# Router logits of the second batch three tiles later, and a new order of the first loads, in a fused attention and mixture-of-experts kernel

## The chip, the cores and the metric

One Trainium2 chip, one of its cores. The number compared is the device time of one execution in microseconds (us). The kernel before took 703.13 us, the median of three runs (702.78 to 705.14). A difference between two versions is read from such runs, and a profile of one execution of each shows where it comes from.

## The reference

Four batches of 512 rows with 512 columns each. First a cross attention whose queries and keys both come from a context `ctx` (so the attention is over context rows) and whose values are the rows of `x` after a layer norm, used along the column axis:

```python
query = einsum('bnc,dc->bnd', ctx, Wq) + bq
key   = einsum('bnc,dc->bnd', ctx, Wk) + bk
attention = softmax(einsum('bnd,bmd->bnm', query, key))
x = x + einsum('bln,bmn->blm', layernorm(x), attention)
h = layernorm(x)
# router: 8 experts, the best 2 of each row, weights renormalised
probs = softmax(h @ gate_w.T);  combine = top2(probs) / sum(top2)
# shared expert of 1408 columns, weighed by its own gate
shared = (silu(h @ sw_gate) * (h @ sw_up)) @ sw_down * sigmoid(h @ shared_gate_w)
# routed experts of 352 columns
moe = sum_e combine[e] * (silu(h @ w_gate[e]) * (h @ w_up[e])) @ w_down[e]
x = x + shared + moe
```

All arrays are float32.

## The kernel before

Every engine has its own instruction stream, written out by hand, and semaphores tie them together; there is no scheduler. An engine works through its stream in order, so a wait holds up all that stands behind it. Large products run as three 16-bit products (`PAIRS`: high by high, high by low, low by high), for which each operand is split into a high half (mostly a copy on ScalarE, ACT) and the remainder (a subtraction on VectorE, DVE).

**The start.** SyncE (SP) issues loads one after the other on its queue: the two projection weights, the rows of batch 0 (`x0_loaded`, 1 MB), the two biases (4 bytes for each of 128 partitions), the router's gate rows (`gw_rows`, 9 rows of 512), the context of batch 1, the rows of batch 1, then the shared expert's weights tile by tile. ACT issues the context of batch 0. TensorE (PE) turns the projection weights and the context (`turn_context`, line 1350), turns the gate rows (line 1472, waits for `gw_loaded`), then projects queries and keys of batch 0 (`project`, line 1357), turns the context of batch 1, and forms the energies (line 1366). DVE meanwhile measures batch 0 (`statistics`, line 900), splits the turned gate rows three ways (lines 1143 to 1152, five small instructions that wait for each other through `gw_step`), normalises batch 0 (line 919, waits for the reciprocal deviation, which GpSimd (POOL) forms at line 591), and then takes the maximum of each energy row (`row_max`, line 930), with which the softmax begins.

**The blocks.** `ffn_block(t)` runs the shared expert on batch t in 11 tiles of 128 columns. On PE each tile j is: the gate product (line 1543, 12 matmuls), the up product (line 1543, 12 matmuls), and the down product of tile j-2 (line 1558, 12 matmuls). ACT forms silu (line 849) and the high half of the hidden tile, DVE the product (line 1271) and the low half. In block 0 ACT and DVE also split the weights of tiles 4 to 10 (lines 826 and 1251), at points listed in `TILES_AT`: tile 8 at (6, "up"), tile 10 at (8, "up"). Tile j's gate product waits for tile j's weights. The staging area holds two tiles, so the load of tile j on SP waits for the split of tile j-2.

**Batch 1 inside block 0.** While block t runs, the attention and routing of batch t+1 are interleaved with it, at points (tile, "gate" | "up" | "down") in tables. For block 0 this is `AT_POINT_FIRST`, which all five engines' streams read; so an entry moves the same stage on PE, ACT and DVE together. At (3, "up") batch 1's normalised rows are split into halves (`halves`). SP then turns the halves by four transposing DMAs into `hT` (`turn_h(1)`, line 506), between the loads of weight tiles 7 and 8. PE's router logits of batch 1 (`router_logits`, line 1420, 32 small matmuls) stand at (5, "up") and wait for all four transposes; nothing before block 1 needs `hT` of batch 1 otherwise. At the same point DVE reads the logits (`read_logits`, lines 993 to 997) and ACT takes the exponential (line 730); at (5, "down") DVE does the routing (`route`, lines 1003 to 1032), whose results are next used in block 1 at (0, "up").

After the four blocks come 39 blocks of routed rows through their experts, which this change does not touch.

Of the kernel before, what the change touches and what calls it, by code (L numbers as in the profile page):

```python
# [13 lines left out]
P = 128  # L14
# [43 lines left out]
    (2, "up"): [("stats2", 0)],  # L58
    (3, "gate"): [("norm2", 0)],
    (3, "up"): [("halves", 0)],  # L60
    (5, "up"): [("logits", 0)],
    (5, "down"): [("route", 0)],
}


# [38 lines left out]
def build_xattn_moe(nc, x, ctx_in, w_q, b_q, w_k, b_k, gate_w, w_gate, w_up, w_down,  # L104
                    sw_gate, sw_up, sw_down, shared_gate_w, out, xs_dram):
    B, S, H = x.shape
    C = ctx_in.shape[2]
    E, _, I = w_gate.shape
    IS = sw_gate.shape[1]
    D = w_q.shape[0]  # L110
    RT = S // P
    KC = H // P
    CC = C // P
    UT = IS // P
    NL = E + 1
# [55 lines left out]
    with ExitStack() as stack:  # L171
        def sb(name, shape, dt):
            return stack.enter_context(nc.sbuf_tensor(name, shape, dt))

        def sem(name):
            return stack.enter_context(nc.semaphore(name))


        bank = [stack.enter_context(nc.psum_tensor(f"bank{i}", [P, 512], F32)) for i in range(8)]
# [7 lines left out]
        def att_bank(b, stage, i):  # L187

            if stage == "h":
                return bank[(2, 0, 1, 3)[i]]  # L190
            if four_banks(b, stage):
                return bank[b * 4 + (2 if stage == "qk" else 0) + i]
            return bank[1] if stage == "assign" else bank[i % 2]
# [62 lines left out]
        def place(b):  # L256
            return borrowed_place if b == 1 else own_place
# [13 lines left out]
        gw_rows = silu_sb[0:NL, :]  # L271
        gw_rest = sb("gw_rest", [P, 2, KC, NL], F32)
        gw3 = sb("gw3", [P, KC, 3, NL], BF16)
        ident = sb("ident", [P, P], F32)
# [10 lines left out]
        logits = sb("logits", [P, RT, NL], F32)  # L285
# [63 lines left out]
        x0_loaded, x1_loaded, x_rest_loaded = sem("x0_loaded"), sem("x1_loaded"), sem("x_rest_loaded")  # L349
        ctx_loaded = sem("ctx_loaded")  # L350
        ctx1_loaded = sem("ctx1_loaded")
        wqk_loaded, bqk_loaded, gw_loaded = sem("wqk_loaded"), sem("bqk_loaded"), sem("gw_loaded")
# [7 lines left out]
        gw_turned, gw_step = sem("gw_turned"), sem("gw_step")  # L360
# [55 lines left out]
        def row_tile(b, i):  # L416
            return rows[b][:, i * H:(i + 1) * H]
# [4 lines left out]
        def _(sp):  # L422
            def load_rows(b, x_sem):
                sp.dma_start(rows[b].rearrange("p (t h) -> p t h", h=H),
                             x[b].rearrange("(t p) h -> p t h", p=P)).then_inc(x_sem, 16)
# [37 lines left out]

            sp.dma_start(wqk[:, 0, :], w_q).then_inc(wqk_loaded, 16)
            sp.dma_start(wqk[:, 1, :], w_k).then_inc(wqk_loaded, 16)
            load_rows(0, x0_loaded)
            sp.dma_start(bqk[:, 0:1], b_q.rearrange("(p a) -> p a", a=1)).then_inc(bqk_loaded, 16)
            sp.dma_start(bqk[:, 1:2], b_k.rearrange("(p a) -> p a", a=1)).then_inc(bqk_loaded, 16)
            sp.dma_start(gw_rows[0:E, :], gate_w).then_inc(gw_loaded, 16)
            sp.dma_start(gw_rows[E:NL, :], shared_gate_w.rearrange("h a -> a h")).then_inc(gw_loaded, 16)  # L470
            sp.dma_start(place(1).ctx_rows, ctx_in[1].rearrange("(t p) c -> p t c", p=P)).then_inc(ctx1_loaded, 16)
            load_rows(1, x1_loaded)

# [419 lines left out]
        def _(dve):  # L893
# [22 lines left out]
            def normalize(which, b):  # L916
                dve.wait_ge(rstd_ready[which], b + 1)
                for i in range(RT):
                    op = nc.vector.tensor_scalar(place(b).normed[:, i, :], row_tile(b, i), mean_var[:, which, i, 0:1],
                                                 rstd[:, which, i:i + 1], ALU.subtract, ALU.mult)  # L920
                    op.then_inc(normed_ready[which], 1)
# [6 lines left out]
            def row_max(b, n):  # L928
                dve.wait_ge(energy_done, RT * b + n + 1)
                nc.vector.tensor_reduce(neg_max[:, n:n + 1], att_bank(b, "energy", n)[:, :], AX.X, ALU.max,  # L930
                                        negate=True).then_inc(max_ready, 1)
# [206 lines left out]
            dve.wait_ge(x0_loaded, 16)  # L1138
            statistics(0, 0)

            gw_ps = bank[5][:, 0:KC * NL].rearrange("p (k e) -> p k e", k=KC)
            dve.wait_ge(gw_turned, 1)
            nc.vector.tensor_copy(gw3[:, :, 0, :], gw_ps).then_inc(gw_step, 1)
            dve.wait_ge(gw_step, 1)
# [5 lines left out]
                                    ALU.subtract).then_inc(gw_step, 1)  # L1150
            dve.wait_ge(gw_step, 4)
            nc.vector.tensor_copy(gw3[:, :, 2, :], gw_rest[:, 1, :, :]).then_inc(gw_step, 1)
            normalize(0, 0)
            row_max(0, 0)
            row_max(0, 1)
            scale_attn(0, 0)
# [183 lines left out]
        def _(pe):  # L1340
            def turn_context(b, c):
                if not first_two(b):
                    if c == 0:
                        pe.wait_ge(ctx_loaded, 16 * b)

                    pe.wait_ge((logits_read, places_read)[c], b)
                elif c == 0:
                    pe.wait_ge((ctx_loaded, ctx1_loaded)[b], 16)
                for i in range(RT):
                    op = nc.tensor.transpose(att_bank(b, "ctx", c)[:, i * P:(i + 1) * P],  # L1350
                                             place(b).ctx_rows[:, i, c * P:(c + 1) * P], ident[:, :])
                op.then_inc(ctx_turned, 1)

            def project(b, i):
                pe.wait_ge(ctxT_ready, CC * b + CC)
                for c in range(CC):
                    op = nc.tensor.matmul(att_bank(b, "qk", i)[:, :], wqkT[:, i, c, :], place(b).ctxT[:, c, :],  # L1357
                                          start=(c == 0), stop=(c == CC - 1))
                op.then_inc(qk_done, 1)
# [9 lines left out]
            def turn_x(b, c):  # L1369
                if c == 0:  # L1370
                    pe.wait_ge(normed_ready[0], RT * b + RT)
                pe.wait_ge(exp_done, RT * b + c + 1)
                for i in range(RT):
                    op = nc.tensor.transpose(att_bank(b, "x", c)[:, i * P:(i + 1) * P],
                                             place(b).normed[:, i, c * P:(c + 1) * P], ident[:, :])
                op.then_inc(x_turned, 1)
# [86 lines left out]
            for i in range(2):  # L1463
                for c in range(CC):
                    op = nc.tensor.transpose(bank[4][:, (i * CC + c) * P:(i * CC + c + 1) * P],
                                             wqk[:, i, c * P:(c + 1) * P], ident[:, :])
            op.then_inc(wqk_turned, 1)
            for c in range(CC):
                turn_context(0, c)
            pe.wait_ge(gw_loaded, 32)  # L1470
            for c in range(KC):
                op = nc.tensor.transpose(bank[5][:, c * NL:(c + 1) * NL], gw_rows[:, c * P:(c + 1) * P],
                                         ident[0:NL, 0:NL])
            op.then_inc(gw_turned, 1)
            pe.wait_ge(wqkT_ready, 1)
            project(0, 0)
            project(0, 1)
            pe.wait_ge(gw_step, 5)
            for c in range(CC):
                turn_context(1, c)  # L1480
            for n in range(RT):
# [3 lines left out]
            project(1, 0)  # L1485
            turn_x(0, 2)
            turn_x(0, 3)
            project(1, 1)
            for c in range(KC):
                turn_attn(0, c)  # L1490
# [182 lines left out]
```

## Time and profile before

| | |
|---|---|
| time, median of three runs | 703.13 us (702.78 to 705.14) |
| the profiled execution's own time | 704.99 us |
| its span, first to last instruction | 703.0 us |
| PE busy | 665.5 us (95%) |
| DVE / ACT / POOL busy | 301.3 / 224.1 / 160.9 us |
| chain that ended last | PE 82%, DVE 7%, DMA 4%, ACT 2% |
| mean granted PE clock | 0.98 of full |

PE is busy nearly throughout, so an interval in which it stands still, or runs at its lower clock, adds to the time unless something else would have held it up anyway. Share of the span says little about single intervals; those are read from the chain of waits and from the timelines of the engines. The stages in us from the span's start: attention of batch 0 to about 48, block 0 to about 160, blocks 1 to 3 to about 458, the experts to the end.

### The profile page before, as it was taken

Reading aid. Unit: us, or ns where it says so; the run is one execution under the profiler, and the core shown is the slowest. Engines: PE = TensorE matmul, PEld = TensorE weight load, DVE = VectorE, ACT = ScalarE, POOL = GpSimd, SP = SyncE. Lnnn points to the kernel's source line nnn. Section 1 sums busy time; section 2 is a strip of 40 time slices with the busy share of each in tenths; the row PEclk is TensorE's granted clock in tenths of the full one; section 3 lists DMA queues with packets and bytes.
Section 4 is the critical chain, followed back from the end, with each engine's and each line's share of the span. In section 5 each row is a group of like instructions: output and inputs, shape, how many; then the busy total and the mean of one; then the engine's idle time right before and its main releaser. Section 6 shows DMA issues by size and latency. Waiting matters only on the chain.

```text
span 703.0 us, 10241 instructions
## 1 busy us (share of the span) xinstructions
PE 665.5 (95%) x3495; PEld 348.4 (50%) x3540; DVE 301.3 (43%) x699; ACT 224.1 (32%) x341; POOL 160.9 (23%) x133
## 2 busy tenths in 40 slices
PE   7989977999999999999999899999999999999991
PEld 5554433444444444444444344456666666666660
DVE  3999544315432536432559763452222222222220
ACT  2545133212630222630445353432222222222220
POOL 2550360003200003200344700012222222222221
PEclk9999997999999999999999999999999999999996
DMA  8530195132530122530167977346566666656632
GB/s 274 187 104 20 49 301 135 50 109 96 147 60 1 28 64 106 137 61 0 36 200 257 310 255 181 94 107 92 92 92 91 92 93 91 93 90 94 90 46 30
DMA packets 116498, 78.29 MB, mean 111 GB/s; under 512 B 79322, under 2 KB 101082, under 8 KB 116451
## 3 DMA queue, kind: packets, MB, share of 16 engines
q1 hardware_dynamic: 104322, 48.77, 28.2%
q0 software_dynamic: 10544, 27.30, 18.1%
q10 hardware_dynamic: 1584, 1.57, 0.7%
q8 instruction: 32, 0.52, 0.3%
q14 instruction: 16, 0.12, 0.1%
HBM read 32.76 MB, written 27.29 MB: 85 GB/s over the span
## 4 chain that ended last, share of the span: by engine, by line
PE 82%; DVE 7%; DMA 4%; ACT 2%; issue 2%; SPq 2%; POOL 1%; ACTq 0%; POOLq 0%
PE bank L1543 26%; PE bank L1591 20%; PE bank L1558 14%; PE bank L1615 10%; PE bank L1400 4%; PE bank L1357 2%; PE bank L1602 2%; PE bank L1366 1%; SPq L506 1%; DMA hT<-L_ffn_w_gate 1%; DVE arena L1245 1%; DMA hT<-hx_odd 1%; DMA silu_sb<-L_ffn_shared_gate_w 1%; DMA out<-staging,token_blk 1%; DVE stats L900 1%
## 5 line engine op out<-in xcount | busy, mean ns | idle before, releaser
L1543 PE MATMUL bank<-hT,arena 128*128 128x512 f16 x1056 | 238.2, 379 | 4.4 <-DVE prod L1271 4.3
L1543 PEld LDWEIGHTS bank<-hT,arena 128*128 128x128 bf16 x1056 | 102.5, 98 | 131.0 <-DVE prod L1271 6.3
L1591 PE MATMUL bank<-arena,hx_odd 128*128 x936 | 152.1, 312 | 0.3 <-issue 0.3
L1558 PE MATMUL bank<-arena,hidden 128*128 128x512 bf16 x503 | 117.8, 384 | 1.4 <-issue 0.2
L1591 PEld LDWEIGHTS bank<-arena,hx_odd 128*128 128x128 f16 x936 | 91.2, 98 | 50.5 <-issue 3.2
L632 POOL DMA_INDIRECT out<-staging,token_blk x39 | 60.6, 1554 | 172.1 <-ACT staging L879 164.0
L1311 DVE TENSOR_TENSOR hidden<-bank,hidden 128x384 bf16<-128x384 f32 x39 | 21.7, 557 | 154.4 <-ACT hidden L871 154.4
L1558 PEld LDWEIGHTS bank<-arena,hidden 128*128 128x128 bf16 x528 | 52.0, 99 | 64.5 <-issue 5.0
L1615 PE MATMUL bank<-arena,hidden 128*128 (+1 forms) x331 | 78.0, 379 | 2.6 <-DVE hidden L1311 1.5
L879 ACT ACTIVATE staging<-bank,w_blk 128x512 f32<-128x512 f32 x39 | 26.8, 687 | 125.6 <-PE bank L1615 125.6
L1271 DVE TENSOR_TENSOR prod<-silu_sb,bank 128x512 f32<-128x512 f32 x44 | 30.1, 684 | 80.4 <-PE bank L1543 74.8
L849 ACT ACTIVATE silu_sb<-bank 128x512 f32<-128x512 f32 x44 | 26.2, 596 | 117.1 <-PE bank L1543 117.0
L843 ACT CAST hidden<-prod 128x512 bf16<-128x512 f32 x44 | 27.0, 618 | 88.2 <-DVE prod L1271 88.2
L1615 PEld LDWEIGHTS bank<-arena,hidden 128*128 128x128 bf16 (+1 forms) x351 | 34.3, 98 | 37.9 <-issue 1.7
L1276 DVE TENSOR_TENSOR hidden<-prod,hidden 128x512 bf16<-128x512 f32 x44 | 35.0, 798 | 28.4 <-ACT hidden L843 28.2
L591 POOL TENSOR_TENSOR rstd<-var_eps,minus_half 128x4 f32<-128x4 f32 x8 | 9.7, 1208 | 155.7 <-DVE var_eps L913 155.5
L1400 PE MATMUL bank<-arena 128*128 128x512 f16 x192 | 43.1, 379 | 0.0
L866 ACT ACTIVATE silu_sb<-bank 128x352 f32<-128x352 f32 x39 | 18.1, 464 | 44.7 <-PE bank L1591 44.7
L1400 PEld LDWEIGHTS bank<-arena 128*128 128x128 f16 x192 | 18.8, 98 | 23.0 <-issue 0.6
L1245 DVE TENSOR_TENSOR arena<-staging,arena 128x1408 bf16<-128x1408 f32 (+1 forms) x14 | 23.5, 1680 | 14.5 <-ACT arena L819 14.2
L819 ACT CAST arena<-staging 128x1408 bf16<-128x1408 f32 (+1 forms) x18 | 25.0, 1395 | 8.8 <-DMA staging<-L_ffn_w_gate 6.5
L1306 DVE TENSOR_TENSOR prod<-silu_sb,bank 128x352 f32<-128x352 f32 x39 | 20.3, 521 | 17.3 <-PE bank L1591 17.3
(183 smaller groups left out, 539.8 us busy)
## 6 DMA issues: line engine op xcount, KB each, us to landing
staging<-L_ffn_w_gate SPq DMA_DIRECT2D x6, 704.0 KB, 4.8
staging<-L_ffn_w_up SPq DMA_DIRECT2D x6, 704.0 KB, 5.7
arena<-x SPq DMA_DIRECT2D x3, 1024.0 KB, 7.9
out<-arena POOLq DMA_DIRECT2D x3, 1024.0 KB, 4.7
staging<-L_ffn_w_down SPq DMA_DIRECT2D x6, 512.0 KB, 4.0
staging<-L_ffn_sw_gate SPq DMA_DIRECT2D x11, 256.0 KB, 3.1
staging<-L_ffn_sw_up SPq DMA_DIRECT2D x11, 256.0 KB, 3.6
staging<-L_ffn_sw_down SPq DMA_DIRECT2D x11, 256.0 KB, 4.5
```

What stands on the lines that cost most here:

```text
L632: nc.gpsimd.indirect_dma_start(out=out[:, :], out_offset=bass.IndirectOffsetOnAxis(ap=token_blk[:, k:k + 1], axis=0), in_=yblk[:, k % 2, : ...
L843: nc.scalar.copy(hidden[:, j % 3, HI, :], prod[:, j % 2, :]).then_inc(hid_hi, 1)
L849: nc.scalar.activation(silu_sb[:, :], gate_ps[:, :], ACT.Silu).then_inc(silu_ready, 1)
L879: nc.scalar.activation(yblk[:, k % 2, :], bank[4 + k % 2][:, :], ACT.Copy, scale=w_blk[:, k:k + 1]).then_inc(y_ready, 1)
L1245: nc.vector.tensor_tensor(arena[:, at + gap:at + gap + n], piece_space[piece_slot(q)][:, 0:n], arena[:, at:at + n], ALU.subtract).then_inc ...
L1271: nc.vector.tensor_tensor(prod[:, j % 2, :], silu_sb[:, :], up_ps[:, :], ALU.mult).then_inc(prod_ready, 1)
L1276: nc.vector.tensor_tensor(hidden[:, j % 3, LO, :], prod[:, j % 2, :], hidden[:, j % 3, HI, :], ALU.subtract).then_inc(hid_lo, 1)
L1400: op = nc.tensor.matmul(att_bank(b, "mix", i)[:, :], place(b).xnT[:, xp, c, i * P:(i + 1) * P], place(b).attnT[:, ap, c, :], start=(c == 0 ...
L1543: op = nc.tensor.matmul(ps[:, :], weights[:, j, wp, kind, c * P:(c + 1) * P], hT[:, t % 2, hp, c, :], start=(c == 0 and s == 0), stop=(c = ...
L1558: op = nc.tensor.matmul(out_ps[i][:, :], hidden[:, j % 3, hp, i * P:(i + 1) * P], weights[:, j, wp, DOWN, :], start=(j == 0 and s == 0), s ...
L1591: op = nc.tensor.matmul(ps[:, 0:I], xT[:, k % X_SLOTS, xp * KC + c, :], arena[:, bass.ds(at + (part_at(0, part) + wp * low_gap(part) + c * ...
L1615: op = nc.tensor.matmul(ps[:, :], hidT[0:n, k % 2, hp, c * P:(c + 1) * P], arena[0:n, bass.ds(at + (DOWN_AT + wp * DN + c * H), H)], start ...
```

## The change

Three edits.

1. In `AT_POINT_FIRST` the entries for batch 1's logits and routing move from tile 5 to tile 8.
2. On PE the first projections (`project(0, 0)`, `project(0, 1)`) stand ahead of the turning of the gate rows, which now go to bank 7 in place of bank 5; the wait for the split gate rows (`gw_step`) moves from ahead of batch 1's context to ahead of `project(1, 1)`, the next user of bank 7. On DVE `normalize(0, 0)` stands ahead of the gate rows' split.
3. On SP the four small loads (two biases, two loads of gate rows) are issued ahead of batch 0's rows.

```diff
-    (5, "up"): [("logits", 0)],
-    (5, "down"): [("route", 0)],
+    (8, "up"): [("logits", 0)],
+    (8, "down"): [("route", 0)],
...
             sp.dma_start(wqk[:, 1, :], w_k).then_inc(wqk_loaded, 16)
-            load_rows(0, x0_loaded)
             sp.dma_start(bqk[:, 0:1], b_q.rearrange("(p a) -> p a", a=1)).then_inc(bqk_loaded, 16)
             sp.dma_start(bqk[:, 1:2], b_k.rearrange("(p a) -> p a", a=1)).then_inc(bqk_loaded, 16)
             sp.dma_start(gw_rows[0:E, :], gate_w).then_inc(gw_loaded, 16)
             sp.dma_start(gw_rows[E:NL, :], shared_gate_w.rearrange("h a -> a h")).then_inc(gw_loaded, 16)
+            load_rows(0, x0_loaded)
...
             statistics(0, 0)
-            gw_ps = bank[5][:, 0:KC * NL].rearrange("p (k e) -> p k e", k=KC)
+            normalize(0, 0)
+            gw_ps = bank[7][:, 0:KC * NL].rearrange("p (k e) -> p k e", k=KC)
             dve.wait_ge(gw_turned, 1)
...
             nc.vector.tensor_copy(gw3[:, :, 2, :], gw_rest[:, 1, :, :]).then_inc(gw_step, 1)
-            normalize(0, 0)
             row_max(0, 0)
...
             for c in range(CC):
                 turn_context(0, c)
-            pe.wait_ge(gw_loaded, 32)
-            for c in range(KC):
-                op = nc.tensor.transpose(bank[5][:, c * NL:(c + 1) * NL], gw_rows[:, c * P:(c + 1) * P],
-                                         ident[0:NL, 0:NL])
-            op.then_inc(gw_turned, 1)
             pe.wait_ge(wqkT_ready, 1)
             project(0, 0)
             project(0, 1)
-            pe.wait_ge(gw_step, 5)
+            pe.wait_ge(gw_loaded, 32)
+            for c in range(KC):
+                op = nc.tensor.transpose(bank[7][:, c * NL:(c + 1) * NL], gw_rows[:, c * P:(c + 1) * P],
+                                         ident[0:NL, 0:NL])
+            op.then_inc(gw_turned, 1)
             for c in range(CC):
                 turn_context(1, c)
...
             turn_x(0, 3)
+            pe.wait_ge(gw_step, 5)
             project(1, 1)
```

The first place is PE in block 0, from batch 1's logits (line 1420) to the end of the block; line 1543 is a tile's gate and up products, line 1558 a down product (x36: the last three). Before:

```order
L1420 MATMUL bank<-gw,hT 128x27 x32
L1558 MATMUL bank<-arena,hidden 128x512 x12
L1543 MATMUL bank<-hT,arena 128x512 x24
L1558 MATMUL bank<-arena,hidden 128x512 x12
L1543 MATMUL bank<-hT,arena 128x512 x24
L1558 MATMUL bank<-arena,hidden 128x512 x12
L1543 MATMUL bank<-hT,arena 128x512 x24
L1558 MATMUL bank<-arena,hidden 128x512 x12
L1543 MATMUL bank<-hT,arena 128x512 x24
L1558 MATMUL bank<-arena,hidden 128x512 x12
L1543 MATMUL bank<-hT,arena 128x512 x24
L1558 MATMUL bank<-arena,hidden 128x512 x36
```

And PE in the same stretch, from the logits to the end of the block, in the changed kernel:

```order
L1420 MATMUL bank<-gw,hT 128x27 x32
L1558 MATMUL bank<-arena,hidden 128x512 x12
L1543 MATMUL bank<-hT,arena 128x512 x24
L1558 MATMUL bank<-arena,hidden 128x512 x12
L1543 MATMUL bank<-hT,arena 128x512 x24
L1558 MATMUL bank<-arena,hidden 128x512 x36
```

Three tiles of products now stand ahead of the logits that stood behind them.

The second place is SP's queue at the start of the program (`arena<-x` is batch 0's rows, then batch 1's; `silu_sb` holds the gate rows, `prod` the context of batch 1):

```order
 L464 DMA arena<-L_xattn_Wq 128x256
 L465 DMA arena<-L_xattn_Wk 128x256
+L466 DMA bqk<-L_xattn_bq 128x1
+L467 DMA bqk<-L_xattn_bk 128x1
+L468 DMA silu_sb<-L_ffn_gate_w 8x512
+L469 DMA silu_sb<-L_ffn_shared_gate_w 1x512
 L424 DMA arena<-x 128x4x512
-L467 DMA bqk<-L_xattn_bq 128x1
-L468 DMA bqk<-L_xattn_bk 128x1
-L469 DMA silu_sb<-L_ffn_gate_w 8x512
-L470 DMA silu_sb<-L_ffn_shared_gate_w 1x512
 L471 DMA prod<-ctx 128x4x256
```

Batch 0's rows are issued four places later.

The third place is DVE at the start, from batch 0's variance to the first row maximum (`gw` and `gw_rest` are the split gate rows, line 919 the normalising):

```order
 L913 TENSOR_SCALAR var_eps<-mean_var 128x4
-L1143 CAST gw<-bank 128x4x9
-L1145 TENSOR_TENSOR gw_rest<-bank,gw 128x36
-L1147 CAST gw<-gw_rest 128x4x9
-L1149 TENSOR_TENSOR gw_rest<-gw_rest,gw 128x36
-L1152 CAST gw<-gw_rest 128x4x9
 L919 TENSOR_SCALAR arena<-arena,mean_var,rstd 128x512 x4
+L1144 CAST gw<-bank 128x4x9
+L1146 TENSOR_TENSOR gw_rest<-bank,gw 128x36
+L1148 CAST gw<-gw_rest 128x4x9
+L1150 TENSOR_TENSOR gw_rest<-gw_rest,gw 128x36
+L1153 CAST gw<-gw_rest 128x4x9
 L930 TENSOR_REDUCE neg_max<-bank 128x1 x2
```

The split of the gate rows moves from between variance and normalising to between normalising and the first row maximum.

## Rows read from the trace of the kernel before

**Rows 1.** Chain of waits, 60 to 165 us: start, us, what.

```profile
104.08 5.76 DMA hT<-hx_odd
...
109.89 1.03 PE bank L1420 x32
110.93 0.22 issue
111.15 4.66 PE bank L1558 x11
...
120.99 2.59 PE bank L1558 x12
```

**Rows 2.** Timeline of PE: start, us, engine, line, what, [idle before <-releaser].

```profile
50.87 0.95 PE L1420 MATMUL bank<-gw,hT 128*128 128x27 bf16 x32
...
109.89 1.03 PE L1420 MATMUL bank<-gw,hT 128*128 128x27 bf16 x32 [8.23 <-DMA hT<-hx_odd]
```

**Rows 3.** Stretches: us, PE busy (x), granted clock, DMA share, GB/s.

```profile
9.40:13.00 3.60, 3.55 (x8) 1.91 (x9) 3.29 (x12) 0.00 (x0) 0.22 (x1) 0.53 1.05 383
111.10:113.00 1.90, 1.85 (x5) 0.75 (x5) 0.58 (x4) 1.21 (x2) 0.00 (x0) 0.50 0.25 86
...
44.50:46.00 1.50, 1.50 (x9) 0.50 1.00 285
```

**Rows 4.** Timeline of SP's queue, 76 to 165 us.

```profile
94.13 12.40 SPq L506 DMA_TRANSPOSE hT<-hx_odd  x4
...
107.75 0.83 SPq L436 DMA_DIRECT2D staging<-L_ffn_sw_down  x1
```

**Rows 5.** DMA issues: KB each, us to landing; from 106.5 to 109, then 4.2 to 5.

```profile
staging<-L_ffn_sw_down SPq DMA_DIRECT2D x1, 256.0 KB, 4.5
...
arena<-x SPq DMA_DIRECT2D x1, 1024.0 KB, 10.1
```

**Rows 6.** Timelines of DVE and ACT, 76 to 165 us.

```profile
113.41 1.76 DVE L1251 TENSOR_TENSOR arena<-staging,arena 128x1536 bf16<-128x1536 f32 x1 [1.66 <-ACT arena L826]
...
119.47 0.18 DVE L1032 TENSOR_TENSOR hx_odd<-chosen,top_inv 128x32 f32<-128x32 f32 x1
121.08 0.69 DVE L1271 TENSOR_TENSOR prod<-silu_sb,bank 128x512 f32<-128x512 f32 x1 [1.43 <-issue]
...
118.93 1.46 ACT L826 CAST arena<-staging 128x1536 bf16<-128x1536 f32 x1
```

**Rows 7.** Timeline of all engines, 0 to 62 us.

```profile
1.72 0.43 SPq L424 DMA_DIRECT2D arena<-x  x1
...
3.69 0.23 SPq L470 DMA_DIRECT2D silu_sb<-L_ffn_shared_gate_w  x1
...
9.45 0.49 PE L1472 MATMUL bank<-ident,silu_sb 9*128 9x9 f32 x4 [2.10 <-DMA silu_sb<-L_ffn_shared_gate_w]
9.60 2.47 DVE L900 BATCH_NORM_STATS2 stats<-arena 128x6 f32<-128x512 f32 x4 [9.60 <-DMA arena<-x]
...
12.60 0.19 DVE L1143 CAST gw<-bank 128x36 bf16<-128x36 f32 x1
12.78 1.05 POOL L591 TENSOR_TENSOR rstd<-var_eps,minus_half 128x4 f32<-128x4 f32 x1 [8.72 <-DVE var_eps L913]
...
13.51 0.18 DVE L1152 CAST gw<-gw_rest 128x36 bf16<-128x36 f32 x1
...
13.86 1.92 DVE L919 TENSOR_SCALAR arena<-arena,mean_var,rstd 128x512 f32<-128x512 f32 x4 [0.17 <-POOL rstd L591]
...
17.06 0.69 DVE L930 TENSOR_REDUCE neg_max<-bank 128x1 f32<-128x512 f32 x1 [1.28 <-PE bank L1366]
...
26.16 2.48 DVE L951 TENSOR_TENSOR arena<-bank,arena 128x512 f16<-128x512 f32 x4 [0.74 <-ACT arena L704]
```

**Rows 8.** DMA queues from 3.5 to 3.9 us: packets, MB, share of 16 engines.

```profile
q10 hardware_dynamic: 149, 0.15, 105.4%
q1 hardware_dynamic: 3, 0.00, 2.2%
```

## The prediction

> **What bounds the kernel now.** I read the page first: PE is busy for 95% of the span and carries 82% of the chain that ended last, so the question is where PE stands still or runs slowly, and whether the edits reach those places. The second view was therefore the chain of waits through block 0. The reader is to see there one transfer, the transposing loads of `hT`, that the chain follows for 5.76 us, then the 32 logits of batch 1, and then a down product of twelve matmuls that takes 4.66 us, where the next one takes 2.59 [rows 1]. The third view, the timeline of PE, gives the stall in full: PE idles 8.23 us ahead of the logits of batch 1, while the logits of batch 0 took 0.95 us and waited for nothing [rows 2]. The fourth, the table of stretches, explains the slow product behind it: the granted clock is 0.50 there, the lower of the two levels, 1.2 GHz, after the idle time [rows 3]. So tile 5 holds one clear loss: a wait, and a cold stretch that the wait leaves behind.
>
> The start is bound otherwise. PE waits 2.10 us for the gate rows [rows 7] and then runs at 0.53 [rows 3]. But by 26.16 us, where DVE takes up the low halves of the attention, the chain has passed to DVE, which is nearly always busy from its first row maximum at 17.06 [rows 7]. What counts at the start is when that first row maximum begins.
>
> **The logits three tiles later.** Before, PE reaches the logits at 109.89 - 8.23 = 101.66 [rows 2], and the down product behind them ends at 111.15 + 4.66 = 115.81 [rows 1]: 14.15 us. Warm and without a wait the two cost 0.95 [rows 2] + 2.59 [rows 1] = 3.54 us. The difference is **10.6 us**: 8.23 of stall, 2.07 of cold down product, 0.3 of cold logits and the gap behind them.
>
> Does the wait come back at the new place? A tile is a gate, an up and a down product, 3 x 2.59 = 7.77 us, so three tiles are 23.3 us and PE arrives at 101.66 + 23.3 = 124.97. Nothing upstream of the transposes moves against the products: but for what the start adds to all of them, SP issues them from 94.13 on as before [rows 4] and they land at 109.85 [rows 1], 15.1 us ahead of PE. The edit gives more delay than the stall needed.
>
> What is late next? Three tiles of products run earlier in time, so their weights must be there. The tightest is tile 8, whose load stands behind the transposes on SP's queue: its last part is issued at 107.75 [rows 4] and lands 4.5 us later [rows 5], at 112.25. ACT's half of the split takes 1.46 us and DVE's 1.76 [rows 6], which makes 115.5. PE reaches the gate product of tile 8 after seven products from 101.66, at 119.8. That leaves 4.3 us. ACT stands at the split for some 5 us with the hidden tile 6 and silu of tile 7 behind it; silu 7 needs a gate product that ends at 114.6, and hidden tile 6 isn't needed before 125.9, so nobody waits for it.
>
> At tile 8 itself the logits end at 124.97 + 0.95 = 125.9. Before, tile 7's split on DVE ended 113.41 + 1.76 - 110.92 = 4.3 us after the logits, and the routing ended at 119.65, 8.7 us after [rows 1, 6]. By the same distances tile 10's weights are ready at 130.2, and PE wants them four products after the logits, at 136.3. The product of tile 9 stands behind the routing on DVE: 134.6 + 0.69 [rows 6] = 135.3, and PE wants it one product later than that, at 138.9. Both fit, with 6.1 and 3.6 us to spare. The routing's results go to block 1, behind two more tiles and the last down products. I cost the moved stage itself at nothing beyond its 0.95 us on PE.
>
> **The start.** The split of the gate rows took 12.60 to 13.69 and lay beside POOL's 1.05 us [rows 7]. Now it stands behind the normalising and lies beside nothing: +1.09 us on DVE. But DVE had 1.28 us of idle time ahead of the first row maximum, waiting for PE [rows 7], and PE loses its 2.10 us wait. With the rows of batch 0 on time, the first row maximum would begin at 13.86 + 1.92 + 1.09 = 16.87, 0.2 us earlier than before.
>
> The rows of batch 0 aren't on time, though. Their issue moves behind four small ones, from an end at 2.15 to one 1.77 us later (3.92 - 2.15) [rows 7]. DVE's whole start hangs on that load, from 9.60 on. From below the delay is 0: between 3.5 and 3.9 SP's queue moved 3 packets while the queue with the context took all the engines [rows 8], so an early issue bought little, and the small loads may use that time. From above it is 1.77. I take 1.0, a bit over the middle, since the rows did begin to move soon after 3.9. The context of batch 1 stands behind the same bytes as before and gets no price.
>
> The Trainium skill speaks against this edit: by its page "DMA: Bandwidth & Descriptors", section "Queues, rings and completion order", the descriptors of one ring are taken in order, so the 256 four-byte pieces of the biases and the gate rows must all be taken up before batch 0's rows. By that rule alone the delay would be the whole 1.77 us or more, and the time about 0.8 us longer than I forecast. The trace agrees as to the order: the gate rows, issued behind batch 0's, came at 9.45, with them. It does not show what the small pieces cost when nothing is ahead of them.
>
> PE now finishes its projections and energies early, and will wait for the first exponentials. Waits of 2.10 and 8.23 us were followed by the lower clock [rows 2, 3, 7]. A cold stretch on the path costs about 2.07 us [rows 1], off the path nothing; PE does little in this stretch that DVE doesn't wait for anyway. I put 0.2 us on it, and keep 0 and 2.07 as its bounds. Sum of the start: -0.2 + 1.0 + 0.2 = **+1.0 us**, between -0.2 and +3.6. DVE and then PE are on the chain without a break from there, so all of it reaches the end.
>
> **The sum.** 10.6 - 1.0 = 9.6 us less. The profiled execution took 704.99 itself (span 703.0 and 2.0 around it), which gives 695.4. It lay 1.86 above the median of the runs, near the slowest of them. One cold stretch more or less is a difference of that size: at 44.5 to 46 the clock was 0.50 as well [rows 3]. From the median the forecast is 703.13 - 9.6 = **693.5 us**.
>
> **The rivals.**
> 1. *The start is dear.* Batch 0's rows come the full 1.77 us late, and PE's idle time ahead of the first exponentials leaves a cold stretch in the projections of batch 1. The start costs 3.6 and the time is 703.13 - 10.6 + 3.6 = 696.1. For it: the 1 MB load is the first thing that DVE waits for. Against it: the projections run beside DVE's work.
> 2. *The stall moves into the weights.* Tile 8's load comes late, and PE waits at its gate product instead. It begins to cost when the load takes over 4.5 + 4.3 = 8.8 us. A load of the start took 10.1 [rows 5], which would cost 1.3 us and, at worst, the same cold stretch: 3.4 of the 10.6, that is 696.9. Against it: 4.5 us was measured while the transposes were still running.
> 3. *Slower than before, by the same place.* ACT takes its work in order. If tile 8's load takes over 8.8 + 9.6 = 18.4 us, PE stands at tile 8 longer than it did at the logits. With a landing after 24 us the wait is 15.2 and the time 703.13 - 9.6 + 15.2 = 708.7. No load in these rows took more than 10.1 us.
> 4. *The edit doesn't remove the wait.* If the transposes came to land when PE asks, not when SP issued them, the stall would go with the logits and only the start would show: 703.13 + 1.0 = 704.1. Against it: PE issues nothing that they wait for after batch 1's halves are ready.
>
> **How the numbers follow.** The forecast has a chance of 0.76, the first rival 0.11, the second 0.07, the third 0.03 and the fourth 0.03. The likeliest case's own range is 692 to 696: the start's bounds, less 0.35 of spread between runs below. The 8-in-10 range is 691.0 to 697.2, which takes in the first two rivals and, below, 1.5 us that a cold stretch fewer (at the start or at 44.5) would give. About what a measurement of this kernel can tell from no change is 0.3%, 2.1 us. Faster by more than that: 0.76 + 0.11 + 0.07 = 0.94. The fourth ends at 704.1, within 0.3%: 0.03 for the same. The third, 708.7, is the 0.03 for slower.
>
> **What would show it.** In the new profile no PE wait of over 1 us between the first down product and block 1, and twelve-matmul down products of 2.59 us throughout; the clock's slice at 105 to 123 us at 9 and not 7. The logits on PE about 3 tiles after the tile-5 products, with no idle time ahead of them. DVE's first statistics at about 10.6 in place of 9.60, the gate rows' split between normalising and the first row maximum, the latter at about 17.9. The forecast is wrong if tile 8's gate product waits for DVE's split, if the logits still wait for `hT`, or if batch 0's rows land after 11.4.

## The result and the profile after

The changed kernel takes 693.99 us (median, 692.27 to 694.44, four runs) against 704.13 for the kernel before (702.78 to 705.23): a ratio of 0.985 with a 95% interval of 0.983 to 0.988. The forecast was 693.5, which is 9.6 us less than the 703.13 that three runs of the kernel before had given; the difference measured is 10.1. The profiled execution took 693.99 itself, its span is 692.1 and was 703.0.

Two lines of the page after, the busy tenths of PE and the granted clock in 40 slices of 17.3 us:

```profile
PE   7989999999999999999998999999999999999991
PEclk9999999999999999999999999999999999999996
```

The slice from 104 to 121 us, in which the kernel before stood still and then ran cold (at the lower of the clock's two levels), is now at 9 on both.

The timeline of PE after, around the logits (start, us, engine, line, what), which answers to [rows 1, 2]:

```profile
118.62 5.34 PE L1543 MATMUL bank<-hT,arena 128*128 128x512 f16 x24
123.80 0.95 PE L1420 MATMUL bank<-gw,hT 128*128 128x27 bf16 x32
124.61 2.75 PE L1558 MATMUL bank<-arena,hidden 128*128 128x512 bf16 x12
127.19 5.34 PE L1543 MATMUL bank<-hT,arena 128*128 128x512 f16 x24
```

No idle time stands ahead of the logits. From one tile's products to the next, with logits and a down product between, it is 127.19 - 118.62 = 8.57 us. The same stretch before, in the timeline of PE:

```profile
96.32 5.34 PE L1543 MATMUL bank<-hT,arena 128*128 128x512 f16 x24
...
115.64 5.34 PE L1543 MATMUL bank<-hT,arena 128*128 128x512 f16 x24
```

That was 19.32 us. The difference, 10.75, is what the moved stage is worth.

What stands on ACT and DVE at the new place, in their timelines after; in brackets the idle time ahead and who ended it:

```profile
112.03 1.47 ACT L826 CAST arena<-staging 128x1536 bf16<-128x1536 f32 x1 [5.56 <-DMA staging<-L_ffn_sw_down]
...
113.53 1.76 DVE L1251 TENSOR_TENSOR arena<-staging,arena 128x1536 bf16<-128x1536 f32 x1 [4.38 <-ACT arena L826]
...
133.30 0.18 DVE L1032 TENSOR_TENSOR hx_odd<-chosen,top_inv 128x32 f32<-128x32 f32 x1
133.52 0.69 DVE L1271 TENSOR_TENSOR prod<-silu_sb,bank 128x512 f32<-128x512 f32 x1
```

ACT does wait for tile 8's load, 5.56 us, and DVE's half of the split ends at 115.29; PE begins that tile's gate product at 118.62, 3.3 us later. The product of tile 9 stands right behind the routing, and nobody waits for it.

The start after, answering to [rows 7], from the timeline of all engines:

```profile
3.35 0.42 SPq L424 DMA_DIRECT2D arena<-x  x1
...
9.75 2.47 DVE L900 BATCH_NORM_STATS2 stats<-arena 128x6 f32<-128x512 f32 x4 [9.75 <-DMA arena<-x]
...
15.85 0.19 DVE L1144 CAST gw<-bank 128x36 bf16<-128x36 f32 x1
...
16.84 1.28 DVE L930 TENSOR_REDUCE neg_max<-bank 128x1 f32<-128x512 f32 x2
...
18.48 1.46 PE L1374 MATMUL bank<-ident,arena 128*128 128x128 f32 x8 [2.12 <-ACT arena L694]
...
19.73 3.39 PE L1357 MATMUL bank<-arena 128*128 128x512 f32 x4
...
26.95 2.48 DVE L951 TENSOR_TENSOR arena<-bank,arena 128x512 f16<-128x512 f32 x4 [1.45 <-ACT arena L704]
```

Batch 0's rows, issued 1.63 us later (3.35 against 1.72), are there at 9.75 instead of 9.60. PE waits 2.12 us for the first exponentials and then runs cold: the granted clock is 0.53 from 19.7 to 23.0, the projection of line 1357 takes 3.39 us, and DVE's low halves begin 0.79 later than before. Yet block 0 starts earlier than before, by 0.9 us. Its first gate product in the timeline of PE, after and before:

```profile
47.38 2.75 PE L1543 MATMUL bank<-hT,arena 128*128 128x512 f16 x12 [0.97 <-DVE hT L963]
```

```profile
48.28 2.75 PE L1543 MATMUL bank<-hT,arena 128*128 128x512 f16 x12
```

Where the 0.79 went, and more, is seen in the timelines of GpSimd (POOL) and DVE, here after:

```profile
29.59 3.10 POOL L586 TENSOR_TENSOR arena<-staging,arena 128x1536 bf16<-128x1536 f32 x1
...
32.27 0.45 DVE L913 TENSOR_SCALAR var_eps<-mean_var 128x4 f32<-128x4 f32 x1
```

and before:

```profile
29.84 3.10 POOL L586 TENSOR_TENSOR arena<-staging,arena 128x1536 bf16<-128x1536 f32 x1
...
31.47 1.49 DVE L913 TENSOR_SCALAR var_eps<-mean_var 128x4 f32<-128x4 f32 x1
```

An instruction of DVE with four elements in each partition, 0.17 us where no split runs beside it, ends when POOL's split of weight tile 1 ends, at 32.7 after and 32.9 before, whenever it began. The start isn't paced by DVE's own work there but by POOL's two splits, which begin with DVE's fourth scaled row (after, that row ends at 23.39 and the first split begins at 23.45; before, 23.63 and 23.70).

### The profile page after: what moved, and what is told of

The parts are those of the page before. It is cut to its first block, busy times and chain, and to the rows that moved or that the text cites. A ratio compares the mean times of both kernels' runs of the same rounds, so it can differ in the third digit from the quotient of the medians.

```text
span 692.1 us, 10286 instructions
## 1 busy us (share of the span) xinstructions
PE 665.4 (96%) x3540; PEld 346.0 (50%) x3540; DVE 300.3 (43%) x699; ACT 224.6 (32%) x341; POOL 160.5 (23%) x133
## 4 chain that ended last, share of the span: by engine, by line
PE 88%; DVE 7%; DMA 2%; issue 1%; ACT 1%; POOL 0%; SPq 0%; POOLq 0%; ACTq 0%
PE bank L1543 30%; PE bank L1591 20%; PE bank L1558 16%; PE bank L1615 11%; PE bank L1400 4%; PE bank L1602 2%; PE bank L1357 2%; PE bank L1366 1%; DMA arena<-x 1%; DVE arena L919 1%; DVE stats L900 1%; DVE arena L1245 1%; DMA out<-staging,token_blk 1%; DVE neg_max L930 0%; DVE stats L1176 0%
## 5 line engine op out<-in xcount | busy, mean ns | idle before, releaser
L1558 PE MATMUL bank<-arena,hidden 128*128 128x512 bf16 x528 | 120.3, 379 | 0.0
L1615 PE MATMUL bank<-arena,hidden 128*128 (+1 forms) x351 | 82.2, 379 | 1.5 <-DVE hidden L1311 1.5
L819 ACT CAST arena<-staging 128x1408 bf16<-128x1408 f32 (+1 forms) x18 | 25.0, 1397 | 10.9 <-DMA staging<-L_ffn_w_gate 7.4
L1306 DVE TENSOR_TENSOR prod<-silu_sb,bank 128x352 f32<-128x352 f32 x39 | 20.3, 521 | 17.3 <-PE bank L1591 17.3
```

The source lines that it names most:

```text
L1558: op = nc.tensor.matmul(out_ps[i][:, :], hidden[:, j % 3, hp, i * P:(i + 1) * P], weights[:, j, wp, DOWN, :], start=(j == 0 and s == 0), s ...
L1615: op = nc.tensor.matmul(ps[:, :], hidT[0:n, k % 2, hp, c * P:(c + 1) * P], arena[0:n, bass.ds(at + (DOWN_AT + wp * DN + c * H), H)], start ...
```

## The experiments

Ratios are to the kernel before, with 95% intervals, from runs on the same chip.

**Only the logits later.** The first edit alone, on the kernel before:

```diff
-    (5, "up"): [("logits", 0)],
-    (5, "down"): [("route", 0)],
+    (8, "up"): [("logits", 0)],
+    (8, "down"): [("route", 0)],
```

> The kernel before with the logits and routing at tile 8, the start as it was. My theory: the whole gain is the wait for the transposes and the cold stretch behind it, so 10.6 to 10.9 us less than before (about 693), no wait on PE ahead of the logits of batch 1, and 2.59 us for the down product behind them. Rival: a good part of the change's gain comes from the start; then this one gains clearly less than the full change, say 8 or under. A cold stretch more or less in either (about 2 us) blurs the difference between single runs.

Measured: 695.3, ratio 0.985 (0.982 to 0.989), that of the full change; no wait ahead of the logits. The rival is out. Its six runs fall into two groups, 693.6 to 693.7 and 696.9 to 697.7. The profile is of the upper one (696.89), and its timeline of the start shows what the old order there can cost:

```profile
10.32 6.63 PE L1357 MATMUL bank<-arena 128*128 128x512 f32 x8
...
18.89 0.69 DVE L930 TENSOR_REDUCE neg_max<-bank 128x1 f32<-128x512 f32 x1 [3.61 <-PE bank L1366]
```

The first projections ran cold throughout (granted clock 0.54 from 10.3 to 16.8) behind a wait of 2.54 us for the gate rows, and the first row maximum waited for PE until 18.89, 1.8 us later than in the profile before.

**Only the start.** The changed kernel with the logits back at tile 5.

> The changed kernel with the logits and routing back at tile 5: only the new order at the start. My theory as predicted: the start costs about 1 us, so 704 to 705; the wait ahead of the logits stays at some 8 us and the down product behind it at 4.66. By the profile of the changed kernel, in which block 0 began 1.0 us earlier than before: 1 us less, about 703. Rival (the start carries the gain): 697 or under.

Measured: 703.93, ratio 0.998 (0.996 to 1.000). The stall is there, in the timeline of PE:

```profile
109.01 1.03 PE L1420 MATMUL bank<-gw,hT 128*128 128x27 bf16 x32 [7.86 <-DMA hT<-hx_odd]
```

The start is worth between nothing and 2.8 us, with no sign of a cost of 1 us. Its down product behind the logits took 3.88, not 4.66: how much of it runs cold differs between these two profiles.

**Tile 6 in place of 8.**

```diff
-    (8, "up"): [("logits", 0)],
-    (8, "down"): [("route", 0)],
+    (6, "up"): [("logits", 0)],
+    (6, "down"): [("route", 0)],
```

> The changed kernel with the logits and routing at tile 6 in place of 8. My theory: the transposes land at a time that doesn't depend on where the logits stand, about 109 us; PE comes to the logits at tile 6 at 100.5 + 7.8 = 108.3, so a wait of 0.5 to 1 us is left, with no fall of the clock, and the time is 0.5 to 1 us above the changed kernel's (694.5 to 695). Rival: the wait moves along with the logits; then 8 us of it and the cold product stay, and the time is 703 or more.

Measured: 694.7, ratio 0.984 (0.981 to 0.987), and no wait at all:

```profile
108.77 0.96 PE L1420 MATMUL bank<-gw,hT 128*128 128x27 bf16 x32
```

The transposes had landed by 108.8 here; my half microsecond was not left, but it was close (with the start alone they landed at 109.01). The landing doesn't move with the logits, and one tile of the three would have done.

**Nothing beside the transposes.** On the kernel before, POOL's stream gets one wait ahead of filling the spare rows and sending batch 0's rows:

```diff
             inverse_deviation(1, 1)
+            pool.wait_ge(hT_in[0], 16 * RT)
             fill_spare()
```

> The kernel before, with GpSimd made to wait for the transposes of batch 1 to have landed before it fills the spare rows and sends batch 0's rows (both of which ran beside the transposes). Theory A: the transposes take 12.4 us to issue because those sends share the DMA engines with them; alone they issue in about 5.4 us, as in block 3, and land at about 103, so that PE waits 1 to 2 us at the logits instead of 8.2 and the time is 6 to 9 us less (694 to 697). Theory B: they are slow by themselves, or by the weight tile ahead of them on the queue; then the wait stays at about 8 and the time at 703 to 705.

Measured: 696.27, ratio 0.987 (0.983 to 0.990). SP's queue and PE, in their timelines (lines after this edit are one higher):

```profile
94.68 7.10 SPq L506 DMA_TRANSPOSE hT<-hx_odd  x4
```

```profile
104.59 0.97 PE L1421 MATMUL bank<-gw,hT 128*128 128x27 bf16 x32 [2.28 <-DMA hT<-hx_odd]
105.41 4.44 PE L1559 MATMUL bank<-arena,hidden 128*128 128x512 bf16 x12
```

Theory A for most of it: the transposes issue in 7.1 us, not in 12.4 [rows 4], and 6 of the 8.2 us of stall go. They were late because POOL's stores ran beside them. The 5.4 us of block 3 didn't come; what holds up the other 1.7 us isn't shown. In this profile, which is of the slowest of the four runs (698.45; the others 695.76 to 696.58), a wait of 2.28 us left most of a cold down product behind it all the same, 4.44 us at a granted clock of 0.59.

**The wait filled.** The changed kernel with 16 transposes of the identity more on PE, between the energies and the first turned rows:

```diff
             for n in range(RT):
                 energy(0, n)
+            for _ in range(16):
+                nc.tensor.transpose(bank[6][:, 0:P], ident[:, :], ident[:, :])
             turn_x(0, 0)
```

> The changed kernel with 16 more transposes of the identity on PE (into a bank that the next projection overwrites) in its wait between the energies and the first turned rows, about 1.7 us of the 2.1. Theory A: the lower clock in the projection of batch 1 (3.4 us where 1.9 is usual) comes from that wait, so the projection is back at 1.9 and the low halves of the attention begin at about 25.7 instead of 26.95; up to 1 us less in time. Theory B: the same as to the clock, but nothing in time (0 plus or minus 0.5), because DVE waits for GpSimd's split of weight tile 1 behind it (its variance of batch 1 ended 32.72, with that split, here and 32.96 before).

Measured: 694.24, ratio 0.985 (0.984 to 0.987). The timeline of PE, then of DVE:

```profile
19.61 1.88 PE L1358 MATMUL bank<-arena 128*128 128x512 f32 x4
```

```profile
25.76 2.48 DVE L952 TENSOR_TENSOR arena<-bank,arena 128x512 f16<-128x512 f32 x4 [0.52 <-ACT arena L705]
...
31.07 1.70 DVE L914 TENSOR_SCALAR var_eps<-mean_var 128x4 f32<-128x4 f32 x1
```

Theory B as to the time. The projection is warm (granted clock 1.00 from 19.6 to 21.4) and DVE comes 1.2 us earlier to its variance, which then takes 1.70 and ends at 32.8, where it ended at 32.7 without the filling. What the warm clock gave, the wait for POOL took. That the filling made the projection warm isn't shown: with the logits at tile 6 the energies ended at the same time as here, PE waited 1.53 us, and the projection took 1.88 without any filling. A second execution of the changed kernel itself says the same of the time. There PE waited 1.23 us and the projection was warm too; DVE's low halves and variance, then PE's first gate product:

```profile
25.70 2.48 DVE L951 TENSOR_TENSOR arena<-bank,arena 128x512 f16<-128x512 f32 x4 [0.52 <-ACT arena L704]
...
31.01 1.70 DVE L913 TENSOR_SCALAR var_eps<-mean_var 128x4 f32<-128x4 f32 x1
```

```profile
47.38 2.75 PE L1543 MATMUL bank<-hT,arena 128*128 128x512 f16 x12 [0.97 <-DVE hT L963]
```

The low halves begin 1.25 us earlier than in the cold profile, and block 0 at the same 47.38.

**Batch 0's rows first again.** The changed kernel without the third edit.

> The changed kernel with the four small loads behind batch 0's rows again (edits 1 and 2 alone). As predicted: batch 0's rows come 1.0 us sooner than with the small loads ahead and the time is about 1 us less. By the profile of the changed kernel, in which batch 0's rows came only 0.15 us later than before: 0.15 less at most, that is no difference. If the gate rows or the biases now come too late for the first projections' outputs (before, the biases landed at 9.0 and 9.9), the energies begin later and nothing is gained.

Measured: 693.74, ratio 0.984 (0.983 to 0.986); the rows came at 9.50. No difference that these runs can tell, as the profile of the changed kernel had it and not as I had predicted.

**The gate rows' split back beside the reciprocal deviation.** The changed kernel with `normalize(0, 0)` behind the split on DVE.

> The changed kernel with the split of the gate rows on DVE back between variance and normalising, beside GpSimd's reciprocal deviation (the turned gate rows are there at 11.9, the variance at 12.9). My theory: the split is hidden again, the first row maximum starts at about 15.8 in place of 16.84, PE's wait ahead of the first turned rows falls from 2.1 to about 1.1 and its clock stays up there. DVE is 1.0 earlier, and the low halves of the attention begin about 1.0 to 2 us earlier than 26.95. Rival: what comes first there doesn't count, because DVE is held up to the end of GpSimd's split of weight tile 1 at about 32.7 in any case, and that split starts with DVE's fourth scaled row; then it's 1.0 less if the split moves along, 0 if not. Time: 1 to 1.5 us less than the changed kernel, about 692.7.

Measured: 693.28, ratio 0.984 (0.982 to 0.985). In its profile batch 0's rows came at 11.55, which no other run showed, and hid the shift; this one stays inconclusive. The first kernel of the last experiment undoes the third edit as well, and there the rows came in time.

**POOL's second split later.**

```diff
             split_unit_tile(0)
-            split_unit_tile(1)
             inverse_deviation(0, 1)
             pool.wait_ge(normed_ready[0], RT * 2)
+            split_unit_tile(1)
             split_unit_tile(2)
```

> The changed kernel with GpSimd's split of weight tile 1 moved behind the reciprocal deviation of batch 1 and its normalising. If DVE's variance of batch 1 (0.45 us here and 1.49 before, 0.17 elsewhere) is held up by that split on GpSimd, it takes 0.17 now and the following row maxima begin 0.3 us earlier than 32.72. Theory A: then the DVE chain to block 0 gets 0.3 us shorter and the time 0.3 less. Theory B: the split, now beside other DVE work, holds up that instead, or the third tile's split comes late, and the time is the same or longer (0 to 3 us).

Measured: 697.95, ratio 0.991 (0.990 to 0.993), 4 us slower than the changed kernel. DVE's and POOL's timelines:

```profile
32.27 0.17 DVE L913 TENSOR_SCALAR var_eps<-mean_var 128x4 f32<-128x4 f32 x1
...
41.46 1.46 DVE L913 TENSOR_SCALAR var_eps<-mean_var 128x4 f32<-128x4 f32 x1
```

```profile
41.43 1.46 POOL L584 CAST arena<-staging 128x1536 bf16<-128x1536 f32 x1
42.97 3.09 POOL L586 TENSOR_TENSOR arena<-staging,arena 128x1536 bf16<-128x1536 f32 x1
46.02 1.01 POOL L591 TENSOR_TENSOR rstd<-var_eps,minus_half 128x4 f32<-128x4 f32 x1
```

Taken away from the first variance, the hold-up appears at the second, which ends with the first half of a split (line 584, to 42.89), and the reciprocal deviation that DVE needs next, at 41.87 in the changed kernel, begins at 46.02. So the collision is with POOL's split and not with anything of DVE's own; and it's no gain to move it.

**Rows first, split beside the reciprocal deviation; and POOL one row earlier.** The second of these two kernels is the first with one number changed:

```diff
-            pool.wait_ge(attn_ready, RT)
+            pool.wait_ge(attn_ready, RT - 1)
             split_unit_tile(0)
```

> The changed kernel with batch 0's rows issued first again and the split of the gate rows back beside GpSimd's reciprocal deviation: of the change, only the logits' place and the first projections ahead of the turned gate rows are left. If the pace of the start is set by GpSimd's split of weight tiles 0 and 1, which begins with DVE's fourth scaled row, everything up to there moves along with the first row maximum: it starts at about 15.6 in place of 16.84, GpSimd's second split and DVE's variance of batch 1 end at about 31.4 in place of 32.7, and the time is 1.2 us less than the changed kernel's, about 692.8. Rival: the start is bound by something I haven't seen; then the variance of batch 1 still ends at about 32.7 and the time is the changed kernel's.

> As e9_rows_first_split_beside, and GpSimd begins its split of weight tiles 0 and 1 after DVE's third scaled row in place of the fourth (about 1.4 us earlier). Theory A (GpSimd's two splits set the pace): DVE's variance of batch 1 ends up to 1.4 us earlier still, about 30, as far as DVE itself is ready (its variance starts at 31.0 less 1.2), so 0.8 to 1.4 us less. Theory B: the first split, now beside DVE's fourth scaled row (a DVE instruction that GpSimd's split holds up, as it holds up the variance), delays that row and the turned rows behind it by up to 3 us, and the time is the same or up to 2 us more.

> The changed kernel itself, beside the two before it, for a comparison on one chip: 692 to 694.5 as before, ratio to the kernel before 0.985.

Measured on one chip: 692.25 for the first, ratio 0.983 (0.980 to 0.985); **689.73** for the second, 0.980 (0.977 to 0.983); the changed kernel 693.15, 0.984 (0.982 to 0.987). All six runs of the second (689.15 to 691.95) lie below all six of the changed kernel (692.21 to 694.43), so it beats both kernels, by about 3.4 and 14.8 us. The runs of the first (690.44 to 693.67) overlap with the changed kernel's, so its gain is read from its profile alone. POOL and DVE in the timeline of the first:

```profile
28.76 3.10 POOL L586 TENSOR_TENSOR arena<-staging,arena 128x1536 bf16<-128x1536 f32 x1
...
30.18 1.70 DVE L913 TENSOR_SCALAR var_eps<-mean_var 128x4 f32<-128x4 f32 x1
```

and of the second:

```profile
21.20 0.92 DVE L946 TENSOR_SCALAR arena<-arena,inv_sum 128x512 f32<-128x512 f32 x1
...
26.58 3.10 POOL L586 TENSOR_TENSOR arena<-staging,arena 128x1536 bf16<-128x1536 f32 x1
...
29.32 0.39 DVE L913 TENSOR_SCALAR var_eps<-mean_var 128x4 f32<-128x4 f32 x1
```

In the first the variance ends at 31.9, with POOL's split again and 0.8 earlier than in the changed kernel, as its row maximum began 0.83 earlier. In the second the split ends at 29.68, 2.2 earlier still: 1.4 by the one row, and 0.86 because batch 0's rows happened to come at 9.05 and not at 9.91. The fourth scaled row (line 946), now beside POOL's first split, took 0.92 for 0.49: theory B's hold-up is there, but small. How much of the 3.4 us is the one row isn't shown: besides the early rows, PE's turning of batch 0's normalised rows (line 1410) took 2.03 us in this profile and 3.58 in the first's.

## Why the prediction was right, point by point

*What bounds the kernel.* Right. The stall at tile 5 and the cold product behind it were the loss, and the rest of block 0 ran on PE without a gap, so all of the gain arrived.

*The logits later.* Predicted 10.6 us, measured 10.75 in the profiles; alone it gives the ratio of the whole change, 0.985. That the landing is a fixed time and not tied to PE's asking, on which the fourth rival depended, is shown by tile 6.

*What is late next.* Predicted for tile 8: landing at 112.25, ready at 115.5, 4.3 us to spare. Measured: ACT took it up at 112.03, ready at 115.29, 3.3 to spare, since PE came a microsecond earlier. The routing ended at 133.48 (134.6 predicted, with the start's delay in it). The second and third rivals didn't occur.

*The start.* The sign was wrong: +1.0 predicted, between nothing and -2.8 measured with the start alone, -0.9 to -1.0 in the profile. Three of its terms:
- *Batch 0's rows 1.0 late* was mis-sized: 0.15 between these two profiles. Over all profiles it is more: with the rows issued first they came at 8.61 to 9.91 (six profiles, median 9.30), with the small loads ahead at 9.75 to 9.81 in six and at 11.55 in a seventh (median 9.76). So the delay is about 0.5 us, between the bounds that I had given. The Trainium skill's rule of ring order (page "DMA: Bandwidth & Descriptors", section "Queues, rings and completion order"), which I had weighed against the edit, would have had 1.77 or more; whether the descriptors were taken in order, no run here shows.
- *The gate rows' split uncovered, 0.2 gained against PE's wait*: the first row maximum was forecast at 16.87 plus the rows' delay and came at 16.84. But the 17.06 of the profile before, from which I counted, is the earliest of three. In the other two profiles with the old start it came at 18.89 (only the logits later) and 17.71 (nothing beside the transposes), each time after a wait for PE; in all six with the whole of the new start it came at 16.84 to 16.90. So the gain is 0.2 to 2.0, and I had sized it on one profile. DVE in the second of those two:

```profile
17.71 0.69 DVE L931 TENSOR_REDUCE neg_max<-bank 128x1 f32<-128x512 f32 x1 [2.91 <-PE bank L1367]
```

- *The cold stretch* came as described (3.39 us for a projection), but the step "DVE and then PE are on the chain without a break from there, so all of it reaches the end" failed. Between them lies POOL's split of weight tile 1, which holds up one DVE instruction to its own end; it took up the 0.79 us. The filled wait and the second execution show it from the other side. What moves the first row maximum itself does pass, since POOL's splits move with it: 0.83 us earlier there is 0.8 earlier at the variance in the first kernel of the last experiment.

Of the 0.9 us by which block 0 begins earlier in the profile, 0.25 came with POOL's splits, which begin at 23.45 instead of 23.70. The rest came from a clock: the stretch in which PE turns batch 0's normalised rows (line 1410) ran at a granted clock of 1.00, before at 0.50. The timelines of PE, after and before:

```profile
43.51 2.02 PE L1410 MATMUL bank<-ident,arena 128*128 128x128 f32 x16 [1.38 <-DVE arena L919]
```

```profile
43.76 3.61 PE L1410 MATMUL bank<-ident,arena 128*128 128x128 f32 x16 [2.41 <-DVE arena L919]
```

That the shorter wait kept the clock up isn't shown. In the second execution of the changed kernel the wait was 2.62 and the stretch took 2.02 all the same; with the start alone the wait was 2.63 and it took 3.34. This part of the gain is spread, not the change's doing. Over the profiles, block 0's first product stands at 48.28 to 49.57 in the three with the old start, and at 47.38 to 47.94 in five with the new one.

*The sum.* 10.75 + 1.0 is 11.8, and the first products of block 1 do stand 11.77 us earlier (147.91 against 159.68). The spans differ by 10.9. The rest is lost in block 3, behind a wait that both have; after:

```profile
381.07 4.45 PE L1543 MATMUL bank<-hT,arena 128*128 128x512 f16 x12 [2.38 <-DVE prod L1271]
```

and before:

```profile
392.83 2.76 PE L1543 MATMUL bank<-hT,arena 128*128 128x512 f16 x12 [2.37 <-DVE prod L1271]
```

The same wait, and this time the clock fell behind it (granted 0.58 against 1.00). That costs 1.69 us, of which 0.75 comes back two tiles later, where the kernel before waits for DVE again (0.57 us at 409.12) and the changed one doesn't. In the second execution of the changed kernel the clock stayed up (2.76 us behind 2.37), so it isn't the change's doing. The forecast of 693.5 was good partly by luck: the start's term was off by 2.0, +1.0 for -1.0, and a loss of 0.9 in block 3, which the forecast didn't have, made up for some of that. The start alone (0.998, 0.996 to 1.000) would not have been clear of the spread; the stage at tile 5 carries the result.

## What to carry to other kernels

An engine that waits for a transfer at a place chosen by hand should be asked how late the work could stand, not only how early; here one tile was enough to end the wait, and the cold stretch behind it was a fifth of the 10.75 us. Before a delay on one engine is carried to the end, look for an engine that holds up the next link anyway: an instruction that is longer than its like, and ends with another engine's, marks one. Read the base of a forecast from more than one profile where the place is unsteady: the first row maximum came at 17.06, 17.71 and 18.89 in three profiles of the old start. Count a stretch that is cold in one profile of a kernel and warm in the next as spread.

## What the runs showed of the hardware

DVE's small `var_eps` took between 0.17 and 1.70 us, and in all twelve profiles in which POOL's second split ran beside it, it ended within 0.03 us of that split. The Trainium skill has the rule on its page "SBUF — State Buffer", section "SBUF: two separate sides": VectorE and GpSimd have one pair of ports in common, and a GpSimd instruction and a VectorE one that uses the pair (in a two-port mode, or with two inputs in SBUF while GpSimd reads SBUF) shut each other out for a whole instruction, whichever starts first. The trace agrees for this instruction, as far as its end goes; in which mode it ran, no trace here shows. DVE instructions that read the matmul results, such as the low halves of line 951, ran beside POOL's splits at their usual length (2.48 or 2.49 us for four in each of these profiles).

The hold-up stands on the chain in one more place. Right ahead of block 0 a scaled row (line 946), 0.49 us elsewhere, takes 1.52 us in the changed kernel (45.12 to 46.64) beside POOL's cast of line 584 (44.89 to 46.35), and block 0's first product waits for what follows it on DVE.

PE's waits of 1.86 (POOL's second split later), 2.10, 2.12 and 2.41 us were followed by the lower clock, at 0.50 to 0.55 of full. Ahead of the same product in block 3 a wait of 2.38 was followed by 0.58 in one execution of the changed kernel, and one of 2.37 by 1.00 in another; one of 2.62 ahead of line 1410 in that other execution was also followed by 1.00. Two executions of one kernel differ by 1.69 us at the product in block 3.

Four transposing DMAs issued in 12.4 us beside GpSimd's stores of spare and routed rows, and in 7.1 with those stores held back.
